# A third layer's gathers, with a wait for landing behind every second quad

## What is computed

```python
h = jnp.maximum(_layernorm(x, axis=-1), 0.0)
...
xj = node_features[col]
s = xj[:, :64]
v = xj[:, 64:].reshape(e, 32, 3)
m0 = s @ Wm_ss * dist * INV8 + jnp.einsum('eui,ei->eu', v, r_vec) @ Wm_vv * (INV_SQRT3 * INV_SQRT32)
m1 = (s @ Wm_sv)[:, :, None] * r_vec[:, None, :] * INV8 + jnp.einsum('eui,uw->ewi', v, Wm_vs) * dist[:, :, None] * INV_SQRT32
...
agg = jax.ops.segment_sum(msg, row, num_segments=n)
```

## Time and profile before

| | us |
|---|---|
| median of 3 runs | 13133.05 |
| lowest and highest | 13108.28, 13135.68 |
| span of the profiled execution | 13146.6 |
| stretch of the third layer's sums in it | 6999 to 8303 |
| busy in the whole span: PE, DVE, POOL, ACT | 9543.0, 8675.6, 7541.7, 4478.5 |

### The profile page before, as it was taken

How to read it: one execution, slowest core, us unless ns; L and a number is a source line. 1 busy time by engine, 2 the same in 40 slices (tenths; PEclk the granted TensorE clock), 3 DMA queues, 4 the chain that set the end, 5 groups by cost and what they waited for, 6 DMA issues and landing times. The chain is left out here.

```text
span 13146.6 us, 247002 instructions
## 1 busy us (share of the span) xinstructions
PE 9543.0 (73%) x62146; PEld 6495.8 (49%) x62147; DVE 8675.6 (66%) x26266; ACT 4478.5 (34%) x14978; POOL 7541.7 (57%) x12370
## 2 busy tenths in 40 slices
PE   4444445458788577777775777787888888888887
PEld 2111111136666444444444555445777777777776
DVE  7666667656666533333334545587889989989987
ACT  0000000015555211111111222104777777777675
POOL 2655566555555455555534666004777777777775
PEclk8666666668888777777776887898999999999998
DMA  4000000012222222222212333680000000000000
GB/s 130 23 21 23 20 24 24 17 32 56 56 57 59 54 56 56 55 55 55 55 44 73 80 81 80 113 159 22 21 21 21 21 21 21 21 21 21 21 21 22
DMA packets 904481, 603.64 MB, mean 46 GB/s; under 512 B 652893, under 2 KB 834355, under 8 KB 901720
## 3 DMA queue, kind: packets, MB, share of 16 engines
q0 software_dynamic: 235616, 359.73, 10.9%
q1 hardware_dynamic: 655992, 203.58, 8.6%
q10 hardware_dynamic: 12480, 35.51, 0.7%
HBM read 518.74 MB, written 79.56 MB: 46 GB/s over the span
## 5 line engine op out<-in xcount | busy, mean ns | idle before, releaser
L1290 POOL DMA_INDIRECT l1s_node_rows<-node_table,l1s_edge_rows x1216 | 1241.2, 1021 | 1144.5 <-DMA l1s_edge_rows<-rows_by_src 690.4
L2366 POOL DMA_INDIRECT l_source_rows<-node_table,l_edge_rows x866 | 854.2, 986 | 982.3 <-DMA l_edge_rows<-rows_by_dst 721.9
L546 PE MATMUL rank<-onehots_and_before,lower_h 128*128 128x427 f16 x812 | 392.8, 484 | 1359.1 <-DVE onehots_and_before L494 688.1
L570 POOL DMA_INDIRECT rows_by_src<-row_s,pos_i x812 | 781.0, 962 | 940.8 <-DVE pos_i L506 684.8
L871 POOL DMA_INDIRECT l_source_rows<-node_table,l_edge_rows x880 | 862.6, 980 | 745.6 <-DMA l_edge_rows<-rows_by_dst 390.2
L1635 POOL DMA_INDIRECT l2s_node_rows<-node_table,l2s_edge_rows x864 | 862.5, 998 | 612.0 <-issue 249.5
L1401 ACT COPY l1s_outer<-l1s_p_outer 128x1024 f32<-128x1024 f32 x304 | 307.6, 1012 | 2035.5 <-remote 1547.8
L570 POOL DMA_INDIRECT rows_by_dst<-row_d,pos_i x812 | 785.1, 967 | 271.2 <-issue 270.6
L1321 DVE TENSOR_TENSOR l_sums_s<-l_sums_s,l1s_p_sums_s 128x8 f32 x1280 | 207.2, 162 | 1060.0 <-remote 697.9
L546 PEld LDWEIGHTS rank<-onehots_and_before,lower_h 128*128 128x128 f16 x812 | 81.8, 101 | 1617.9 <-issue 1075.3
L494 DVE TENSOR_REDUCE onehots_and_before<-onehots_and_before 128x427 f16<-128x2135 f16 x202 | 861.9, 4267 | 21.9 <-issue 19.7
(11 more groups left out here) (553 smaller groups left out, 28930.3 us busy)
## 6 DMA issues: line engine op xcount, KB each, us to landing
l_xv_by<-h_turned_l SPq DMA_DIRECT2D x120, 320.0 KB
l_source_rows<-node_table,l_edge_rows POOLq DMA_INDIRECT x1746
l_xs_by<-h_turned_l SPq DMA_DIRECT2D x40, 640.0 KB
l1s_edge_rows<-rows_by_src SPq DMA_DIRECT2D x1216, 19.5 KB
l1s_node_rows<-node_table,l1s_edge_rows POOLq DMA_INDIRECT x1216
rows_by_src<-pad_rows_s ACTq DMA_DIRECT2D x16, 1053.0 KB
l2s_edge_rows<-rows_by_src SPq DMA_DIRECT2D x216, 78.0 KB
l_edge_rows<-rows_by_dst SPq DMA_DIRECT2D x220, 72.0 KB
```

Source lines behind the costliest of these rows:

```text
L570: pool.indirect_dma_start(rows_, bass.IndirectOffsetOnAxis(ap=pos_i[:, k, o, t:t + 1].bitcast(U32), axis=0), tile[:, k, t, :], None).then_ ...
L1290: pool.indirect_dma_start(xg[q][:, s, :], None, table, bass.IndirectOffsetOnAxis(ap=pay[q][:, s, S_DST:S_DST + 1].bitcast(U32), axis=0)).t ...
L2366: pool.indirect_dma_start(xg[u][:, s, :], None, K["table0"], bass.IndirectOffsetOnAxis(ap=pay[u][:, s, D_SRC:D_SRC + 1].bitcast(U32), axis ...
```

## The change

Behind the four gathers of each quad with odd k, GpSimd waits until `xg_in[k]` shows that all four have landed, and raises `pool_seen`. Nothing else differs.

```diff
@@ -1634,6 +1634,9 @@
                         for s in range(QUAD):
                             pool.indirect_dma_start(xg[k][:, s, :], None, table,
                                                     bass.IndirectOffsetOnAxis(ap=pay[k][:, s, S_DST:S_DST + 1].bitcast(U32), axis=0)).then_inc(xg_in[k], 16)
+                        if k % 2 == 1:
+                            pool.wait_ge(xg_in[k], 16 * QUAD * it + 16 * QUAD)
+                            pool.sem_inc(pool_seen, 1)
                 for k in range(AHEAD):
                     pool.wait_ge(xg_in[k], 16 * QUAD * ITERS)
```

## The result

The changed kernel takes 13222.2 us (median of 5 runs, 13207.1 to 13263.3) against 13133.05 us for the kernel before (median of 5, 13108.3 to 13146.4). The ratio is 1.0072, with a 95% interval of 1.0054 to 1.0090: 89 us slower, where 83 had been forecast.

What follows compares the result with a forecast made beforehand. GpSimd, with 12% slack, was taken as the stage's path: gathers 862.5, short gaps 234.4, new gaps 278.2 and tail 10.4 make 1385.5 us against 1302.6, +83, so 13133 becomes 13216 us; range 13115 to 13305.

Steps and rivals of the forecast that it cites:

- GpSimd has little slack and becomes the path: Stage L1635 to L1692: GpSimd has only 12% of slack over bare issuing, and nothing stands in front of it afterwards.
- Length of one gap: GpSimd's pause at each added wait: 2.6 us in place of 0.31, bounds 1.77 and 3.4; 107 gaps make 278.2 us.
- Landing as ScalarE sees it: Part of the gap: end of a gather's descriptor work to ScalarE's start on the landed rows, 1.77 us.
- GpSimd's restart behind it: Part of the gap: GpSimd wakes 0.75 to 0.76 us after ScalarE; the sum of 2.53 is rounded up to 2.6.
- Short gaps: GpSimd's gaps between gathers where no new wait stands: 756 of 0.31 us, 234.4 us.
- Gathers: GpSimd's 864 gathers in the stage: 862.5 us, mean 998 ns, taken as unchanged.
- Tail: From the last gather to the stage's end: only the last quad is left, 10.4 us against 39.1 before.
- The slow stretches go with the pause: TensorE's crawls, read as caused by many gathers in a row, end; GpSimd's 149.7 us of stops at `summed` go.
- Rival A, faster: GpSimd restarts with ScalarE (gap 1.77 us) and every gather takes 947 ns: -50 us, 13083 us; chance 9%.
- Rival C, the crawl stays: TensorE's slow stretches remain and the waits come on top of each five-quad cycle: +248 us, 13381; chance 10%.
- Rival D, the clock: TensorE, idling between quads, stays at 1.2 GHz and becomes the bound: about +190 us, 13323; chance 3%.
- The sign in the profile: If right, GpSimd's idle time before L1635 is near 510 us, put down mostly to the landing of `l2s_node_rows`.

## Why the prediction was right

- **GpSimd has little slack and becomes the path: right.** (The 12% are 149.7 of 1263.5 us; over the bare issuing it is 13%.) The two stages of the changed kernel, 1.5 us apart on chips whose stages of before are 160 us apart, show it.
- **Length of one gap: forecast 2.6 us, measured 2.77.** Landing as ScalarE sees it was right, 1.76 us on average over the 107 gaps. GpSimd's restart behind it was 1.01 instead of 0.76 + 0.07. That the difference is the waits which now stand behind the landing is a reading; no run took them away. Over 107 gaps the term came out at 296.3 us instead of 278.2, +18.
- **Short gaps: 241.0 us (537.3 - 296.3) instead of 234.4, +7.** Eleven of them last 1.27 us, one every 72 gathers, on both kinds of chip. The kernel before has no gap over 0.6 us where there are no slow stretches. Why they come with the change is open.
- **Gathers: 848.5 us instead of 862.5, -14.** I had held the mean at 998 ns; it fell to 982. The traces show why. Most gathers take 0.95 us whatever VectorE does, but 152 in the kernel before take 1.24 us on average, and each of the 152 overlaps VectorE's second product (L1683). In the changed kernel there are 94 of 1.24 us, again every one beside that product (now L1686), and 58 fewer at 0.29 us more make 17 us. With a wait behind every quad only 36 are left, which is the 21 us missing there. So the term was not "unchanged": the pauses shift the gathers away from that product. Overlap alone doesn't lengthen one: 119 short gathers of the changed kernel overlap it too.
- **Tail: 13.1 us instead of 10.4, +3.** The term missed that `add` runs four quads behind `build`, so four pairs of additions are left at the end, started every 1.86 us:

```profile
8381.06 1.52 DVE L1695 TENSOR_TENSOR l_sums<-l_sums,l2s_p_sum 128x512 f32 x2 [1.14 <-PE l2s_p_sum L1668]
...
8382.92 1.51 DVE L1695 TENSOR_TENSOR l_sums<-l_sums,l2s_p_sum 128x512 f32 x2 [0.35 <-DVE l_sums L1695]
8384.77 1.52 DVE L1695 TENSOR_TENSOR l_sums<-l_sums,l2s_p_sum 128x512 f32 x2 [0.34 <-DVE l_sums L1695]
8386.63 1.51 DVE L1695 TENSOR_TENSOR l_sums<-l_sums,l2s_p_sum 128x512 f32 x2 [0.34 <-DVE l_sums L1695]
```

The four differences, +18 + 7 - 14 + 3, make the 13 us by which the stage, 1398.9, missed 1385.5. That 83 and 89 us lie so close is in part luck: the gathers, taken as unchanged, gave back half of what the gaps cost more, and in the profiled executions the stage alone is 96 us longer and the whole 101. The two spans differ by 5 us more, which lie outside the stage: it starts 10 us earlier, and what follows it takes 15 us longer.

- **The slow stretches go with the pause: right**, and it is what made the sum right: without it the waits cost 258 us. The reading of the cause, many gathers in a row, now has its runs: 8 and 12 in a row show no stops, 16 do, and a pause of another sort does the same as the change's. That the stops come from the slow stretches is shown best by the kernel before on a chip without them, which has neither.
- **Rival A, faster:** the gathers did get shorter, by 16 ns of the 51 it needed, but the gap was a full us above its 1.77.
- **Rival C, the crawl stays:** it didn't, in either kernel with a pause behind every second quad.
- **Rival D, the clock:** TensorE starts many pairs at 1.2 GHz: in the timeline above half a quad takes 3.36 us, from 7308.01 to 7311.37, at a granted clock of 0.52, and then 1.72 at 1.00. But the stage's mean is 0.83, the two quads take some 9 us and GpSimd gives TensorE 12.8. The rule of the Trainium skill (TensorE: Matmul & The Clock Gate, section on HAM oscillation) that pieces cut up by waits for data start at the low clock is seen in part: in 66 of the 108 pairs of quads the first four passes take over 1.1 us (1.4 at the low clock, 0.78 at the high one), in 42 they start at the high clock. As argued it costs the stage nothing.
- **The sign in the profile:** idle time near 510 us, "put down mostly to the landing". The time came, 537.3 us; the label didn't, it reads "issue".
- By the Trainium skill's fit (DMA: Bandwidth & Descriptors, section on the anatomy of one DMA on the GpSimd path) a landing would have come an estimated 2.2 us after the gather's start; the trace of the changed kernel has 2.77 from 7307.03 to ScalarE's start at 7309.80. The measurement decides: it was right to build on the row.

## What to carry to other kernels

Before adding a wait, write out the budget of the engine that waits: its busy time, its short gaps and its stops. If the stops are shorter than the new waits together, the engine becomes the bound, and its plain sum gives the new time; here it did so on both kinds of chip, though the old time depended on something unexplained.

A wait of GpSimd for its own gathers costs the landing plus its own restart, here 2.8 us, and a wait on something long past cost nothing that could be measured. Where only a break is wanted, fewer pauses (every third quad here) do the same.

## What the runs showed of the hardware that was not expected

The same program ran 15% slower on one kind of chip than on the other (13133 against 11409 us). The difference lies ahead of the stage, whose first gather starts at 6999.2 against 5406.3, and in the stage, 1302.8 against 1142.7; what follows it takes 4845 and 4853 us. Ahead of the stage, too, GpSimd issues gathers and scatters, 3720 in all.

TensorE can start passes only every 2 us or so, in the middle of a quad and with its operands there, while GpSimd issues gathers without a break. A break of about 2.8 us in GpSimd's issuing after 8 or 12 gathers prevents it; after 16 it doesn't. A wait for the landing isn't needed for that, though in every break that was tried the gathers did land.

The trace takes two suspects away. Here is what each DMA queue moved (packets, MB, share of the 16 engines), first in the whole stage of the kernel before, then in the crawl of the earlier trace rows, 7043.0 to 7070.7, then in the fast stretch from 7073.2 to 7088.1:

```profile
q0 software_dynamic: 41472, 84.99, 24.1%
q1 hardware_dynamic: 112932, 17.10, 7.9%
q8 instruction: 1, 0.02, 0.0%
q14 instruction: 2, 0.02, 0.0%
```

```profile
q0 software_dynamic: 898, 1.81, 24.6%
q1 hardware_dynamic: 1584, 0.24, 5.1%
```

```profile
q0 software_dynamic: 487, 1.02, 24.3%
q1 hardware_dynamic: 2112, 0.32, 13.1%
q8 instruction: 1, 0.02, 0.5%
q14 instruction: 1, 0.01, 0.1%
```

Three packets of instructions in 1303 us, and none in the crawl: the engines aren't waiting for instructions to be loaded by DMA. And a packet of the gathers' queue takes as long in the crawl as in the fast stretch (27.7 us x 16 x 24.6% / 898 is 121 ns, 14.9 us x 16 x 24.3% / 487 is 119), so the DMA engines aren't slower at them either. Why some chips do this and others don't, and what it is that the gathers hold up in TensorE, stays open.
